# The second graph layer on one core: x is kept by SyncE, copies stand ahead of norms on ScalarE, norms come three places later

## What is computed

```python
x = x + _L0_gnn_ref(_layernorm(x), adj, W, b)         # a_norm @ x @ W.T + b
x = x + _L0_ffn_ref(_layernorm(x)[None], ...)[0]      # mixture of 8 experts, top 2
x = x + _L1_gnn_ref(_layernorm(x), adj, W, b)         # relu(a_norm @ x @ W + b)
x = x + _L1_ffn_ref(_layernorm(x)[None], ...)[0]      # LN, attention, x + attention, LN, experts
```

## Time and profile before

| | us |
|---|---|
| median of 3 runs (lowest, highest) | 2963.14 (2962.2, 2964.66) |
| the profiled execution, own time | 2960.15 |
| its span | 2958.5 |
| PE busy | 2472.5 (84%) |
| DVE busy | 1993.0 (67%) |
| ACT busy | 1573.0 (53%) |
| POOL busy | 1251.6 (42%) |
| mean granted TensorE clock | 0.915 |

### The profile page before, as it was taken

One profiled execution on the slowest core, in us unless ns is written; L12 is line 12 of the kernel. 1 busy time (PEld: TensorE's weight loads), 2 busy tenths in 40 slices (PEclk: granted clock), 3 DMA queues, 4 the chain that ended last, 5 costly groups with the idle time before them and its releaser, 6 DMA issues. The chain is left out here.

```text
span 2958.5 us, 54884 instructions
## 1 busy us (share of the span) xinstructions
PE 2472.5 (84%) x20856; PEld 1919.4 (65%) x20856; DVE 1993.0 (67%) x2987; ACT 1573.0 (53%) x2652; POOL 1251.6 (42%) x738
## 2 busy tenths in 40 slices
PE   4789805999997998758999999999999997409992
PEld 3668704999995877644666666666666664409992
DVE  5775424888877865438777777777777773328883
ACT  4554304777764543323666666666666665206761
POOL 0001051000004402234888888888888886230003
PEclk9999957999998999876999999999999999559996
DMA  9988115666646753224000000220000000126663
GB/s 398 362 309 341 47 67 193 230 229 238 240 162 217 235 185 129 97 90 122 14 16 10 14 16 16 46 48 16 10 14 16 10 12 1 46 83 223 241 232 105
DMA packets 118767, 375.96 MB, mean 127 GB/s; under 512 B 22256, under 2 KB 56432, under 8 KB 100656
## 3 DMA queue, kind: packets, MB, share of 16 engines
q1 hardware_dynamic: 96192, 302.78, 28.9%
q0 software_dynamic: 20800, 65.82, 6.0%
q10 hardware_dynamic: 1584, 4.75, 0.4%
HBM read 314.30 MB, written 58.98 MB: 126 GB/s over the span
## 5 line engine op out<-in xcount | busy, mean ns | idle before, releaser
L1255 POOL TENSOR_TENSOR at_pool_sum<-at_pool_sum,at_probs 128x1024 f32<-128x1024 f32 x364 | 866.7, 2381 | 97.0 <-ACT at_probs L1381 55.7
L1410 DVE TENSOR_REDUCE at_part_max<-ps_x 128x2 f32<-128x1024 f32 x624 | 734.4, 1221 | 228.1 <-PE ps_x L1311 227.8
L1381 ACT ACTIVATE at_probs<-ps_s 128x512 f32<-128x512 f32 x1352 | 698.4, 603 | 323.3 <-PE ps_s L1270 292.8
L1270 PE MATMUL ps_s<-at_qst,at_kst 97*128 97x256 f32 x2704 | 517.6, 311 | 5.2 <-ACT at_probs L1381 4.0
L1270 PEld LDWEIGHTS ps_s<-at_qst,at_kst 97*128 97x128 f32 x2704 | 368.9, 189 | 218.5 <-ACT at_probs L1381 127.2
L1287 PE MATMUL ps_oz<-at_probs,k_xhat 128*32 128x256 f32 (+1 forms) x5408 | 391.4, 386 | 0.0
L570 PE MATMUL ps_acc<-adj_hi,y_hi 128*128 128x512 f32 (+1 forms) x728 | 290.1, 399 | 93.6 <-DMA k_bias<-bias 32.8
L636 DVE TENSOR_TENSOR adj_lo<-adj_raw,adj_hi 128x1024 fp32r<-128x1024 f32 (+1 forms) x182 | 208.7, 1148 | 184.1 <-ACT adj_hi L410 181.7
L1040 POOL DMA_DIRECT2D results<-ex_res x54 | 39.3, 727 | 645.4 <-DVE ex_res L1027 645.4
L571 PE MATMUL ps_acc<-adj_lo,y_hi 128*128 128x512 f32 (+1 forms) x728 | 278.1, 382 | 0.0
L572 PE MATMUL ps_acc<-adj_hi,y_lo 128*128 128x512 f32 (+1 forms) x728 | 277.9, 382 | 0.0
(11 more groups left out here) (201 smaller groups left out, 4047.6 us busy)
## 6 DMA issues: line engine op xcount, KB each, us to landing
ex_w<-w SPq DMA_DIRECT2D x108, 1024.0 KB, 6.8
adj_raw<-adjT SPq DMA_DIRECT2D x156, 512.0 KB, 4.9
k_xhat<-adj SPq DMA_DIRECT2D x26, 1664.0 KB, 8.6
slots<-zeros POOLq DMA_DIRECT2D x27, 512.0 KB, 24.2
ex_rows<-slots SPq DMA_DIRECT2D x54, 256.0 KB, 2.9
results<-ex_res POOLq DMA_DIRECT2D x54, 256.0 KB, 2.8
at_qst<-qk_parts SPq DMA_DIRECT2D x78, 128.0 KB, 2.5
ex_b<-b SPq DMA_DIRECT2D x54, 128.0 KB, 2.1
```

The costliest lines, as they stand in the source:

```text
L1255: pool.tensor_tensor(pool_sum[:, g % 2], pool_sum[:, g % 2], probs[:, tile % RING], ALU.add).then_inc(pool_added, 1)
L1270: last = pe.matmul(ps_s[:, unit % S_BANKS, hh, :], kst[:, 2 * j + hh, k * P:(k + 1) * P], qst[:, g % 2, 2 * j + hh, :], start=True, stop=True)
L1381: act.activation(probs[:, tile % RING, 2 * j:2 * j + 2], ps_s[:, unit % S_BANKS], ACT.Exp, scale=scale).then_inc(taken, 1)
L1410: dve.tensor_reduce(part_max[:, g % 2, heads, qt, kc], ps_x[:, pair, :], AX.X, ALU.max).then_inc(x_free, 1)
```

## The change

`keep` moves from POOL to SP, at position `turns[c] + 11`, with two semaphores in turn. The second layer's applies, second norm, turns, produces, lifts and splits all stand three positions later. On ACT `round_product` and `copy_turned` (in the first layer the logits and the copy) come right behind the rounding of the piece, ahead of evacuation, roots and applies, in both layers. The norms' semaphore counts are renumbered, since the first norm of chunk c + 1 now comes before the second norm of chunk c. In the first layer PE waits for the parameters at its first `times_w` and not at its start.

```diff
-    applies = at_positions([(at + 10 + q, p) for at, c, p, q in pairs])
-    roots2_begin, roots2_end = ... turns[c] + 12 ... turns[c] + 13
-    applies2 = at_positions([(at + 14 + q, p) for at, c, p, q in pairs])
+    applies = at_positions([(at + (10 if first else 13) + q, p) for at, c, p, q in pairs])
+    keeps = at_positions([(turns[c] + 11, c) for c in range(CHUNKS)])
+    roots2_begin, roots2_end = ... turns[c] + 15 ... turns[c] + 16
+    applies2 = at_positions([(at + 17 + q, p) for at, c, p, q in pairs])
+    norms = sorted((turns[c] + (15 if second else 8), second, c) for c in range(CHUNKS) for second in range(1 if first else 2))
+    norm = {(c, second): n for n, (_, second, c) in enumerate(norms)}
...
-        turned_at = at_positions([(at + 12 + 3 * q, p) for at, c, p, q in pairs])
-        copied_at = at_positions([(at + 16 + 3 * q, p) for at, c, p, q in pairs])
+        turned_at = at_positions([(at + 15 + 3 * q, p) for at, c, p, q in pairs])
+        copied_at = at_positions([(at + 19 + 3 * q, p) for at, c, p, q in pairs])
...  (produced 13 to 16, taken 17 to 20, split 18 to 21)
-            keep(0)
             for c in range(CHUNKS):
                 add_output_bias(c)
-                if c + 1 < CHUNKS:
-                    keep(c + 1)
                 for k in chunk_tiles(c):
                     store(k)
...
+            def keep(c):
+                at = slice(first_tile(c), first_tile(c + 1))
+                sp.wait_ge(chain, at.stop)
+                sp.dma_start(m.x_kept[...], m.x[:, at, :]...).then_inc(x_kept[c % 2], 16)
+            for g in range(len(jobs) + PAST_END):
+                if g < len(jobs):
...
+                if not first:
+                    for c in keeps(g):
+                        keep(c)
...
+                for n in taken_at(g):
+                    take_logits(n) if first else round_product(n)
+                for p in copied_at(g):
+                    copy_turned(p)
                 for c in evacuations(g):
                     evacuate(c)
...
-                        act.wait_ge(x_kept, 16 * c + 16)
-                        apply(p, m.x, m.x, normed, 2 * c + 1)
+                        act.wait_ge(x_kept[c % 2], c // 2 * 16 + 16)
+                        apply(p, m.x, m.x, normed, norm[c, 0] + 1)
...
-                for n in taken_at(g):
-                    take_logits(n) if first else round_product(n)
-                for p in copied_at(g):
-                    copy_turned(p)
...
                 if p:
                     pe.wait_ge(taken, 2 * p)
+                elif first:
+                    pe.wait_ge(params_loaded, 16 * 7)
...
-            if first:
-                pe.wait_ge(params_loaded, 16 * 7)
```

More of the change, by code:

```diff
@@ L250, in graph_layer @@
     roots_begin, roots_end = at_positions([(turns[c] + 8, c) for c in range(CHUNKS)]), at_positions([(turns[c] + 9, c) for c in range(CHUNKS)])
-    applies = at_positions([(at + 10 + q, p) for at, c, p, q in pairs])
-    roots2_begin, roots2_end = at_positions([(turns[c] + 12, c) for c in range(CHUNKS)]), at_positions([(turns[c] + 13, c) for c in range(CHUNKS)])
-    applies2 = at_positions([(at + 14 + q, p) for at, c, p, q in pairs])
+    applies = at_positions([(at + (10 if first else 13) + q, p) for at, c, p, q in pairs])
+    keeps = at_positions([(turns[c] + 11, c) for c in range(CHUNKS)])
+    roots2_begin, roots2_end = at_positions([(turns[c] + 15, c) for c in range(CHUNKS)]), at_positions([(turns[c] + 16, c) for c in range(CHUNKS)])
+    applies2 = at_positions([(at + 17 + q, p) for at, c, p, q in pairs])
+    norms = sorted((turns[c] + (15 if second else 8), second, c) for c in range(CHUNKS) for second in range(1 if first else 2))
+    norm = {(c, second): n for n, (_, second, c) in enumerate(norms)}
     if first:
@@ L259, in graph_layer @@
     else:
-        turned_at = at_positions([(at + 12 + 3 * q, p) for at, c, p, q in pairs])
-        copied_at = at_positions([(at + 16 + 3 * q, p) for at, c, p, q in pairs])
-        produced_at = at_positions([(at + 13 + 3 * q + i, 2 * p + i) for at, c, p, q in pairs for i in range(2)])
-        taken_at = at_positions([(at + 17 + 3 * q + i, 2 * p + i) for at, c, p, q in pairs for i in range(2)])
-        split_at = at_positions([(at + 18 + 3 * q + i, 2 * p + i) for at, c, p, q in pairs for i in range(2)])
+        turned_at = at_positions([(at + 15 + 3 * q, p) for at, c, p, q in pairs])
+        copied_at = at_positions([(at + 19 + 3 * q, p) for at, c, p, q in pairs])
+        produced_at = at_positions([(at + 16 + 3 * q + i, 2 * p + i) for at, c, p, q in pairs for i in range(2)])
+        taken_at = at_positions([(at + 20 + 3 * q + i, 2 * p + i) for at, c, p, q in pairs for i in range(2)])
+        split_at = at_positions([(at + 21 + 3 * q + i, 2 * p + i) for at, c, p, q in pairs for i in range(2)])
     G = 2 * HG
@@ L283, in graph_layer @@
         lifted = s("qk_lifted")
-        x_kept, qk_kept, split = s("x_kept"), [s("qk_kept0"), s("qk_kept1")], s("qk_split")
-        m.pool_dma.extend([x_kept] + qk_kept + come)
+        x_kept, qk_kept, split = [s("x_kept0"), s("x_kept1")], [s("qk_kept0"), s("qk_kept1")], s("qk_split")
+        m.pool_dma.extend(qk_kept + come)
     with ExitStack() as ctx:
@@ L324, in _ @@
                 return
[L326 to L329, removed]
             def add_output_bias(c):
@@ L373, in _ @@
                 sp.dma_start(wv[:], t["wv"]).then_inc(wide_loaded, 16)
[L374 to L381, removed]
+            def keep(c):
+                at = slice(first_tile(c), first_tile(c + 1))
+                sp.wait_ge(chain, at.stop)
+                sp.dma_start(m.x_kept[:, at.start * D:at.stop * D], m.x[:, at, :].rearrange("p t d -> p (t d)")).then_inc(x_kept[c % 2], 16)
+            for g in range(len(jobs) + PAST_END):
+                if g < len(jobs):
+                    c, pc = jobs[g]
+                    if first and c in (0, 2) and 2 * pc + 2 + c // 2 < NT:
+                        load_rows(2 * pc + 2 + c // 2)
+                    if g >= raw_ring:
+                        sp.wait_ge(lo_made, g - raw_ring + 1)
+                    n = PIECE * WIDTHS[c]
+                    src = t["adjT"][c * PIECES + pc] if WIDTHS[c] == RCHUNK else t["adjT_tail"][pc]
+                    sp.dma_start(raw[:, g % raw_ring, 0:n], src).then_inc(loaded[g % raw_ring], 16)
+                if not first:
+                    for c in keeps(g):
+                        keep(c)
         @block.scalar
@@ L420, in root @@
                 at = slice(first_tile(c), first_tile(c + 1))
-                n = which + (c if first else 2 * c)
-                act.wait_ge(moments, n + 1)
+                act.wait_ge(moments, norm[c, which] + 1)
                 act.activation(m.roots[:, 0, at], m.guarded[:, 0, at], ACT.Sqrt).then_inc(rooted, 1)
@@ L488, in _ @@
                     if first:
-                        apply(p, m.x, m.xhat, normed, c + 1)
+                        apply(p, m.x, m.xhat, normed, norm[c, 0] + 1)
                     else:
-                        act.wait_ge(x_kept, 16 * c + 16)
-                        apply(p, m.x, m.x, normed, 2 * c + 1)
+                        act.wait_ge(x_kept[c % 2], c // 2 * 16 + 16)
+                        apply(p, m.x, m.x, normed, norm[c, 0] + 1)
                 if not first:
@@ L496, in _ @@
                     for p in applies2(g):
-                        apply(p, m.x, m.xhat, normed2, 2 * (2 * p * P // RCHUNK) + 2)
-                for n in taken_at(g):
-                    take_logits(n) if first else round_product(n)
-                for p in copied_at(g):
-                    copy_turned(p)
+                        apply(p, m.x, m.xhat, normed2, norm[2 * p * P // RCHUNK, 1] + 1)
         @block.tensor
@@ L711, in _ @@
                 for c in roots_end(g):
-                    end_root(c, c + 1 if first else 2 * c + 1)
+                    end_root(c, norm[c, 0] + 1)
                 if not first:
@@ L719, in _ @@
                     for c in roots2_end(g):
-                        end_root(c, 2 * c + 2)
+                        end_root(c, norm[c, 1] + 1)
             counts.settle(dve)
```

## The result

Median 2938.91 us of 4 runs (2938.02 to 2941.36) against 2963.64 us (2962.2 to 2964.66): ratio 0.9918, 95% interval 0.9901 to 0.9935, 24.7 us faster. Forecast were 2929.6 and a gain of 33.5; the time lies inside the range of 2912 to 2946. The profiled execution has a span of 2939.7 us after 2958.5.

A forecast was written before the change was run, and what follows sets the result against it. Bound: the second layer's loop through PE's tiles, the late store of x, apply and copy. Landmarks gave 31.7 us, the first layer 1.8, together 33.5: 2929.6 us against the median 2963.14; range 2912 to 2946.

The forecast's parts named there:

- What bounded the kernel: Second layer: PE's tiles, late store of x on POOL, apply and copy form a loop; ACT waits 38.7 us.
- PE's cycle, the chain and the start: Second layer: PE 31.5 or 23.5 us a chunk, ACT-DVE hand-overs 31.3 or 26.9; chunk 0's first tile at 1110.9.
- parts 1 and 2: Second layer: keep on SP removes the 38.7 us wait; ACT's new order makes an ACT-DVE chain of 31.3 or 26.9.
- Part 3: POOL's bias addition meets busy DVE in the second layer: 1.5 us a cycle, 1.1 with half-wide pieces; bounds 0 and 2.1.
- Part 4: Second layer three positions later: early pieces PE would do anyway; ten tiles, not eight, stand behind the last piece.
- The landmarks: PE's start of each chunk's first tile, second layer, summed to an end at 1287.3 against 1319.0: gain 31.7 us.
- B: Second layer: late copies make PE wait at half clock, additions cost full 2.1; 3.5 us more per cycle, 2944; chance 0.21.
- A: Second layer: POOL's additions slip into gaps, ACT-DVE chain stays under PE; four cycles save 12 us, 2918; chance 0.15.
- C: Second layer: ACT-DVE chain outgrows the old loop; decides from 38.7 us a cycle, 2972 at 41; chance 0.03.
- D: Second layer: ACT's wait stays, as SP itself sits behind the ring and keep comes no sooner; about 2962; chance 0.03.
- the signs: Second layer: no x_kept wait, copy waits under 15 us, first-tile spacings about 33 and 28, last split near 1286.
- The first layer: Copy ahead of the root removes two late produces of 0.89 us, 1.8; removing PE's parameter wait gives nothing.

The follow-up runs named there:

- e4: Kernel before with, in the second layer, only the keep moved to SP; first layer's changes included: 2914.92 us, ratio 0.9846 to the kernel before.
- e8: Full change, but the keep back on POOL, behind the bias addition of the chunk before: 2953.95 us, ratio 0.9968 to the kernel before.
- e1: Full change, but POOL's seven bias additions taken out of the loop and made as one at attention's start: 2924.01 us, ratio 0.9881 to the kernel before.
- e3: Full change, but second layer's old positions instead of three later; keep on SP and new ACT order stay: 2916.71 us, ratio 0.9851 to the kernel before.
- L: Not a run: the part of the change that puts the second layer's applies, second norm, turns and products three positions later.
- e11: Full change, but second layer's old positions, and POOL's bias additions made as one in attention: 2915.34 us, ratio 0.9839 to the kernel before.
- e7: Full change, but the first layer as before, with old ACT order and the parameter wait at PE's start: 2942.88 us, ratio 0.9929 to the kernel before.
- e5: Full change, but POOL's bias addition of a chunk behind that chunk's second store: 2939.32 us, ratio 0.9917 to the kernel before.
- e9: Full change, but POOL's bias addition ahead of the last store of the chunk before: 2927.59 us, ratio 0.9872 to the kernel before.

## Why the prediction was right, and where it was off

**What bounded the kernel**, and that the keep frees it: right, shown by e4 and e8. The keep costs nothing on SP: ACT waited for a piece of the matrix once in the second layer, 1.0 us.

**PE's cycle, the chain and the start**: right in sum. I had chunk 0's first tile at 1110.9; it is at 1110.40, though the stretch began 1.2 us earlier than before. What parts 1 and 2 give without POOL shows in e1: the four cycles come within 0.8 us of the forecast, but single ones miss by up to 2.0 to either side, which cancels by luck. That the chain of ACT and DVE sets the half-wide cycle was not tested by itself. Spacing of the first tiles, us:

| chunks | forecast without POOL | e1 | forecast | after |
|---|---|---|---|---|
| 0 to 1 | 31.5 | 32.0 | 33.0 | 32.0 |
| 1 to 2 | 28.9 | 30.9 | 30.4 | 35.6 |
| 2 to 3 | 26.9 | 27.0 | 28.0 | 31.2 |
| 3 to 4 | 26.9 | 25.1 | 28.0 | 30.0 |
| sum | 114.2 | 115.0 | 119.4 | 128.8 |
| tail | 57.0 | 58.0 | 57.0 | 60.1 |

**Part 3 is the step that failed, in size.** I put POOL's addition at 1.5 and 1.1 us a cycle, 5.2 in the four; it cost 13.8 in them (128.8 less 115.0), all of it in the last three (4.7, 4.2 and 4.8), and about 2 more in the tail. Its upper bound of 2.1 a cycle was too low as well. Three things were missed: DVE lost 3 us per addition in these three cycles and not 2.1, since the held split had started 0.7 to 0.8 us ahead of the addition; the loss fell ahead of a take and a lift, where PE had no slack; and the blocks of PE behind the waits ran partly at half clock, 2.81 to 3.65 us for 1.95. The other 2.5 us that the stretch lacks stand in e1 as well: 0.8 in its cycles, 1.0 in its tail and 0.7 up to chunk 0's first tile. The Trainium skill ("SBUF — State Buffer", section "Who interferes with whom") says that a DVE instruction with two SBUF inputs contends with a GpSimd one that reads SBUF, and that the loser is fully blocked. The traces agree for large splits, which made next to no progress until the addition's end (4.28 us for 1.22). I had weighed that rule against a row with one small instruction, and the rule was the better guide. The hold begins ahead of the addition's recorded start, which the rule does not give.

**Part 4 was read too kindly.** "At the start PE does pieces it would have done anyway" is true, but it is three positions with full pieces, and chunk 0's first tile comes 11.0 us later (1099.43 in e3, 1110.40 after). With POOL out of the way L costs 9.4 us (e11 to e1, 218.2 to 227.6): the first tile is 11.0 us later there too, and from it to the end e1 is only 1.6 us shorter (173.0 after 174.6). That the pieces done early are missing later, where PE had room beside the ACT-DVE chain, fits this but was not shown. With POOL in it costs 17.8 to 22.6, because L also turns a harmless addition into an expensive one. The landmarks priced the change as a whole and never asked what each part was worth, so they could not show that the three places worked against the keep.

**The rivals.** B (2944, every copy late, the addition at its full price) came within 5.1 us, closer than the forecast, which missed by 9.3. It had the addition right; the late copies it shared the price with did not happen (PE's wait for them is 12.0 us, in e1 too). A fell with the addition. C and D did not happen; by C's own terms 41 us a cycle give 2974 and not 2972. Of the signs, x_kept, the copies (12.0) and the first two cycles' start (32.0) came as named, and the spacing of chunks 3 and 4 (30.0 for 28) and the last split (1298.5 for 1286) did not. **The first layer**: 1.8 forecast, 1.9 by the two profiles; nothing at the start, as forecast. e7 puts it higher, at 3.5 by its profile and 4.0 by the medians.

**In sum**: 33.5 forecast; 18.6 in the stretch and 1.9 in the first layer in one profile each. The medians show 24.7, the two profiled executions 18.8 (2960.15 less 2941.36): the one of before was 3.5 below its median, the one of after 2.5 above it. So 6 us between the medians' gain and that of the profiles are scatter between executions; 9 us of the forecast gain are missing by the medians, 13 by the stretch. The time lies inside the range because the range reached as far as rival B; the stretch, which is what the sum added up, gave 18.6 of its 31.7 us.

## What to carry to other kernels

When an engine's wait is removed, the work that used to fall into other engines' idle time beside it meets them busy: list it, and price it at its full length in front of the heaviest position, not at the mean. Measure a change's parts one by one even when the whole is faster: here the store's move gave 38.9 us of the stretch, and the shift by three places took 18 to 23 back. And a later place in a software pipeline can be paid twice: the stage comes later (9.4 us here), and other work falls beside it (the rest).

## What the runs showed that I had not expected

- A DVE instruction with two SBUF inputs was held from before POOL's addition started, when that addition stood directly behind a DMA issue: 0.79 us ahead of it after (1143.69 and 1144.48), 0.87 in e5 (1126.77 and 1127.64). In both, the DVE instruction that began first was the one held. Whether the issue ahead of the addition or the recorded start of POOL's instruction accounts for this is open; e9, with no issue directly ahead, had no split that began before the addition and so doesn't tell. A DMA issue alone did not hold it: in e4 the half-wide splits that begin at 1173.52 and 1175.81, beside two stores' issues, took their usual 0.69 us.
- The output bias as one addition of 128x6656 took 14.24 us, less than the seven in the loop (6 x 2.4 and 1.27, 15.7).
- The kernel with only the keep moved in the second layer (e4) is 24 us faster than the full change, 22 if each is compared with its own batch.
